# Rows and marks of batches 0 and 1 moved to GpSimd inside attention, and one square root placed three transfers later

## The reference, cut to what matters

```python
# B = 4 batches of N = 256 tokens, D = 256; 32 heads of 8; 32 experts, top 6, hidden width 176
x = x + tanh(g_xattn) * xattn(layernorm(x), ctx)     # rotary q and k, softmax over 256 keys, @ Wout + bout
x = x + tanh(g_ffn) * ffn(layernorm(x))
def ffn(flat):                                       # 1024 tokens
    shared = sum(relu(flat @ sw1[e] + sb1[e]) @ sw2[e] + sb2[e] for e in range(2)) / 2
    logits = flat @ router_w + router_b
    topk_p, topk_i = top_k(softmax(logits), 6);  topk_p /= topk_p.sum()
    routed = sum(gate[:, e] * (relu(flat @ rw1[e] + rb1[e]) @ rw2[e] + rb2[e]) for e in range(32))
    return shared + routed
```

## Time and profile before

| | us |
|---|---|
| median of 3 runs | 388.41 (388.39 to 388.55) |
| the profiled execution | 387.09 |
| its span, first to last instruction | 385.3 |
| busy: TensorE, VectorE, ScalarE, GpSimd | 333.4, 240.6, 214.6, 221.7 |

### The profile page before, as it was taken

The page is one execution under the profiler, slowest core; times in us unless marked ns, Lnnn a source line. Parts: engine busy times, 40 slices in busy tenths (PEclk is TensorE's granted clock), DMA queues, the critical chain, the costliest instruction groups (busy, mean ns, idle before and its releaser), DMA issues.

```text
span 385.3 us, 8620 instructions
## 1 busy us (share of the span) xinstructions
PE 333.4 (87%) x2574; PEld 262.3 (68%) x2574; DVE 240.6 (62%) x753; ACT 214.6 (56%) x537; POOL 221.7 (58%) x267
## 2 busy tenths in 40 slices
PE   8889999999899988786772999999999999999800
PEld 5567766666666664564541898999999999999700
DVE  7997788789789888569310355555555545445426
ACT  4795899979878877232130455555555555555400
POOL 8466332103013456757774288888788888787830
PEclk9999999999999999699786899999999999999965
DMA  7799999996004014613233488888888888897688
GB/s 227 208 309 310 308 326 315 320 237 205 4 2 134 19 60 125 204 60 117 101 116 125 128 125 144 137 151 138 139 146 147 142 143 141 138 146 108 76 195 282
DMA packets 63295, 62.20 MB, mean 161 GB/s; under 512 B 6258, under 2 KB 61588, under 8 KB 63252
## 3 DMA queue, kind: packets, MB, share of 16 engines
q1 hardware_dynamic: 48532, 44.60, 40.5%
q0 software_dynamic: 13680, 17.05, 27.4%
q10 hardware_dynamic: 1040, 0.01, 0.2%
HBM read 29.01 MB, written 32.63 MB: 160 GB/s over the span
## 4 chain that ended last, share of the span: by engine, by line
PE 55%; DVE 12%; issue 10%; POOL 9%; DMA 8%; ACT 5%; SPq 0%; POOLq 0%; DVEq 0%
PE psum L1608 14%; PE psum L1590 10%; POOL rows_by_block L502 7%; PE psum L1301 6%; PE psum L1348 5%; DVE nmax L906 5%; DMA sum<-ob,xs 5%; PE psum L1581 4%; PE psum L1599 3%; ACT probs L625 2%; PE psum L1319 2%; PE psum L1196 2%; PE psum L1282 2%; PE psum L1401 2%; POOL sum L546 2%
## 5 line engine op out<-in xcount | busy, mean ns | idle before, releaser
L546 POOL DMA_INDIRECT sum<-ob,xs x79 | 122.4, 1549 | 40.1 <-DVE ob L1166 26.9
L906 DVE TENSOR_REDUCE nmax<-psum 128x2 f32<-128x512 f32 x128 | 80.9, 683 | 13.2 <-PE psum L1301 12.3
L1608 PE MATMUL psum<-w,hT 88*128 (+1 forms) x316 | 81.5, 380 | 0.0
L625 ACT ACTIVATE probs<-psum 128x512 f32<-128x512 f32 x128 | 69.5, 599 | 15.3 <-PE psum L1319 13.8
L1166 DVE TENSOR_SCALAR ob<-psum,gate 128x256 f32<-128x256 f32 x79 | 38.2, 484 | 53.5 <-PE psum L1608 38.1
L755 ACT ACTIVATE hT<-psum,b1b 88x128 f32<-88x128 f32 x158 | 48.8, 357 | 35.6 <-PE psum L1599 34.6
L1590 PE MATMUL psum<-w,xT 128*128 x316 | 61.6, 318 | 0.3 <-ACT xT L746 0.3
L1608 PEld LDWEIGHTS psum<-w,hT 88*128 88x128 f32 (+1 forms) x316 | 53.8, 190 | 4.6 <-issue 0.3
L746 ACT ACTIVATE xT<-psum 128x256 f32<-128x256 f32 x79 | 30.3, 384 | 46.3 <-PE psum L1581 46.2
L502 POOL DMA_INDIRECT rows_by_block<-Vx,slot x48 | 47.6, 991 | 14.4 <-issue 14.1
L425 POOL CAST Qx<-nmax 128x8 fp32r<-128x8 f32 x32 | 6.3, 197 | 74.2 <-DVE nmax L906 74.1
(11 more groups left out here) (194 smaller groups left out, 468.6 us busy)
## 6 DMA issues: line engine op xcount, KB each, us to landing
rows_by_block<-blank SPq DMA_DIRECT2D x1, 10744.0 KB, 38.2
xs<-rows_by_block SPq DMA_DIRECT2D x79, 136.0 KB, 2.9
w<-in_L_ffn_rw_dram SPq DMA_DIRECT2D x2, 2816.0 KB, 22.1
w<-in_L_ffn_rw_dram SPq DMA_DIRECT2D x16, 352.0 KB
sum<-blank SPq DMA_DIRECT2D x3, 1152.0 KB, 13.4
w<-sum SPq DMA_DIRECT2D x12, 256.0 KB, 5.3
sum<-ob,xs POOLq DMA_INDIRECT x79
x_sb<-in_x_dram SPq DMA_DIRECT2D x4, 256.0 KB, 3.9
```

What stands on the lines that cost most here:

```text
L546: pool.indirect_dma_start(yd[i], bass.IndirectOffsetOnAxis(ap=xs[b % ROWS_AHEAD][:, X_ID:X_ID + 1].bitcast(U32), axis=0), ob[i][:, :], Non ...
L625: act.activation(probs[g % 2][:, :, n, :], st_bank(g, n)[:, :].rearrange("p (t q) -> p t q", t=TB), ACT.Exp, scale=SCALE).then_inc(exp_ok, 1)
L906: dve.tensor_reduce(nmax[i % 2][:, :, n], S_BANK[(4 * i + n) % SB][:, :].rearrange("p (t k) -> p t k", t=TB), AX.X, ALU.max, negate=True). ...
L1608: ins = pe.matmul(Y_BANK[b % 2][:, 0:D], hT[b % 2][0:rows, c, :], w2[0:rows, bass.ds(expert[b], 1), c, :].rearrange("p a n -> p (a n)"), s ...
```

## The change: what it does

In attention, for batches 0 and 1:

- The two normalised row tiles are made by GpSimd (`row_early`): the first right behind the Newton step at step 16 + 8b, the second behind the maxima of the next step. VectorE's two L945 at step 18 + 8b are gone.
- ScalarE copies the router's scores out of `T_BANK` into `lg` (`scores_copied`, semaphore `raw_ok`) ahead of its exponentials of step 21 + 8b. TensorE's next `transposes` waits for this copy and no longer for VectorE's sum. VectorE adds the bias from `lg` to `lg`.
- `mask` is made by GpSimd in three additions (`mask_early`, behind the maxima of step 22 + 8b, after a wait on `ch_ok`). VectorE's reduction L971 is gone, and so is its wait on its own `chosen`.
- The transfers inside attention are one fewer: step 30 issues one in place of two, and step 31 issues numbers 4 and 5 in place of 5 and 6.
- After attention, transfers 18, 19 and 20 stand ahead of the inverse root of batch 3, not behind it.

```diff
...
-            DEALT_AT = {28: (0, 2), 29: (2, 3), 30: (3, 5), 31: (5, 7)}
+            DEALT_AT = {28: (0, 2), 29: (2, 3), 30: (3, 4), 31: (4, 6)}
...
+                pool.wait_ge(nstep_ok, b + 1)
+                row_early(TB * b)
+
+            def row_early(n):
+                pool.wait_ge(pv_mm, NG)
+                pool.tensor_scalar(xrow[:, n, 0:D], x_sb[:, n, :], mv[:, n, 0:1], rstd[:, n:n + 1],
+                                   ALU.subtract, ALU.mult).then_inc(xn2_ok, 1)
+
+            def mask_early(b):
+                rows = slice(TB * b, TB * b + TB)
+                c = chosen[b]
+                some = halfsum[:, :, :, :]
+                pool.wait_ge(ch_ok, b + 1)
+                then(pool.tensor_tensor(some, c[:, :, 0:TOPK // 2, :], c[:, :, TOPK // 2:TOPK, :], ALU.add))
+                then(pool.tensor_tensor(mask[:, rows, :], some[:, :, 0, :], some[:, :, 1, :], ALU.add))
+                pool.tensor_tensor(mask[:, rows, :], mask[:, rows, :], some[:, :, 2, :], ALU.add).then_inc(mask_ok, 1)
...
+                    if g == NG * b + 17:
+                        row_early(TB * b + 1)
                     if g == NG * b + 21:
                         marks_of(b)
+                    if g == NG * b + 22:
+                        mask_early(b)
...
+            deal(EACH + EACH // 2, EACH + EACH // 2 + 3)
             inverse_root(B + 3, slice(NT - TB, NT))
-            deal(EACH + EACH // 2, NT * TOPK)
+            deal(EACH + EACH // 2 + 3, NT * TOPK)
...
+                if i - 1 in SCORE_STEPS:
+                    scores_copied(SCORE_STEPS[i - 1])
...
+            def scores_copied(b):
+                act.wait_ge(lg_mm, b + 1)
+                act.activation(lg[:, TB * b:TB * b + TB, :], C_LG[b].rearrange("p (t e) -> p t e", t=TB), ACT.Copy).then_inc(raw_ok, 1)
...
             def scores(b):
-                dve.wait_ge(lg_mm, b + 1)
-                dve.tensor_tensor(lg[:, TB * b:TB * b + TB, :], C_LG[b].rearrange("p (t e) -> p t e", t=TB),
+                if b < EARLY:
+                    dve.wait_ge(raw_ok, b + 1)
+                    src = lg[:, TB * b:TB * b + TB, :]
...
-                    if (at, part) == (18, 0):
-                        dve.wait_ge(nstep_ok, b + 1)
-                        dve.wait_ge(pv_mm, NG)
-                        normalised_row(TB * b)
-                    if (at, part) == (18, 2):
-                        normalised_row(TB * b + 1)
...
-                        then(choice_of(b))
-                    if (at, part) == (23, 0):
-                        mask_of(b)
+                        choice_of(b).then_inc(ch_ok, 1)
...
                 if i - AHEAD - 1 in SCORE_STEPS:
-                    pe.wait_ge(lg_ok, SCORE_STEPS[i - AHEAD - 1] + 1)
+                    pe.wait_ge(raw_ok, SCORE_STEPS[i - AHEAD - 1] + 1)
```

More of the change, by code:

```diff
@@ L166, in gated_cross_attention_moe @@
         roundup = blank[:, P:P + NE]
+        halfsum = placed[:, 0, :, :].rearrange("p k e -> p (k e)")[:, 0:TB * TOPK * NE // 4].bitcast(BF16).rearrange(
+            "p (t k e) -> p t k e", t=TB, k=TOPK // 2)
         HS_AT = 6 * H * HR
@@ L223, in gated_cross_attention_moe @@
             sem(n) for n in ("dif_ok", "ex_ok", "mask_ok", "masks_ok", "rk_mm", "row_ok", "slot_ok", "dealt"))
+        raw_ok, ch_ok = sem("raw_ok"), sem("ch_ok")
         nstep_ok, at8_ok, exp_row_ok, rk_ok, had_ok, upto_ok, placed_ok, pool_placed = (
@@ L942, in normalised_rows @@
                 normalise_rows(b, xrow[:, TB * b:TB * b + TB, 0:D], xn2_ok)
-            def normalised_row(n):
-                dve.tensor_scalar(xrow[:, n, 0:D], x_sb[:, n, :], mv[:, n, 0:1], rstd[:, n:n + 1],
-                                  ALU.subtract, ALU.mult).then_inc(xn2_ok, 1)
             def scores(b):
-                dve.wait_ge(lg_mm, b + 1)
-                dve.tensor_tensor(lg[:, TB * b:TB * b + TB, :], C_LG[b].rearrange("p (t e) -> p t e", t=TB),
+                if b < EARLY:
+                    dve.wait_ge(raw_ok, b + 1)
+                    src = lg[:, TB * b:TB * b + TB, :]
+                else:
+                    dve.wait_ge(lg_mm, b + 1)
+                    src = C_LG[b].rearrange("p (t e) -> p t e", t=TB)
+                dve.tensor_tensor(lg[:, TB * b:TB * b + TB, :], src,
                                   rtb_sb[:, :].unsqueeze(1).to_broadcast([P, TB, NE]), ALU.add).then_inc(lg_ok, 1)
```

## The result

| | before | after |
|---|---|---|
| median of the executions measured side by side, 20 each | 386.53 (383.21 to 389.02) | 388.94 (387.05 to 394.46) |
| the same, a second time (run g1, 23 and 12) | 387.58 | 388.08 (386.36 to 392.74) |
| the profiled execution, its span | 387.09, 385.3 | 387.26, 385.5 |
| mean granted clock of TensorE in the profiled execution | 0.948 | 0.959 |

The ratio of after to before is 1.0061, 95% interval [1.0036, 1.0087], and in the second measurement 1.0025 [0.9993, 1.0058]. The change cost between 0.25 and 0.6%, and by the second measurement alone a loss is not shown. From the 388.41 at which the prediction started, the first ratio gives 390.8 and the second 389.4, where 387.2 and "faster" were forecast. The ratios leave out the executions that took over 1.5% more than the quickest of the same kernel, among them the three of the changed kernel over 394.

What follows compares the result with a forecast made beforehand. The 79 blocks start only when all 48 transfers have landed, so time follows the last transfer. Attention 1.6 earlier, less one more transfer and a later root, put transfer 24 1.2 earlier: 388.41 - 1.2 = 387.2, range 386.2 to 389.0.

Steps and rivals of the forecast that it cites:

- The sum at step 31: All attention terms added at GpSimd's maxima of step 31: 1.6 earlier than 146.72.
- 18 to 19, rows gone from VectorE: Attention: two L945 leave VectorE, so TensorE's scores start 0.2 earlier.
- 21, the copy: Step 21: ScalarE's copy fits its idle time and removes TensorE's 0.84 wait; 0.7 gained (bounds 0.4 and 0.84).
- 23 and 24, the mask: VectorE loses L971 and comes earlier to the residual TensorE waits for; 0.4 gained.
- 24 to 26, wait for `had_ok`: VectorE stands still 1.2 ahead of the scan, having saved 0.64 by the rows; 0.6 lost.
- 28 to 31, batch 1: Steps 29 to 31: missing mask (0.7) and earlier residual (0.2) bring the maxima of step 31 0.9 earlier.
- Steps 24 to 26: the rows on GpSimd: Each row takes 0.95 (bounds 0.73 and 1.87); the second, ahead of the rounding, delays `had_ok`; 0.6 lost.
- rival A: GpSimd, steps 24 to 26: rows are slow, up to 1.87, sign turning at about 1.5; 389.4, chance 0.13.
- The transfers: After attention: one more follows (+1.28), the root starts at 169.4, transfer 24 goes 1.2 earlier, at 175.87.
- the new wait: GpSimd ahead of transfer 24: it waits about 1.3 for `slot` of batch 2, ready at 175.5.
- B: Steps 24 to 26: a row takes 0.4 to 0.5, the wait for `had_ok` hardly exists; 386.6, chance 0.17.
- C: Attention hardly gets faster, ScalarE having little idle time: 0.6 in place of 1.6; 388.2, chance 0.22.

Runs made afterwards that it cites:

- g1: The changed kernel measured again, nothing altered, against the kernel before; ratio 1.0025 [0.9993, 1.0058].
- e8: The kernel before with only ScalarE's copy of the router's scores added, TensorE waiting for that copy; ratio to before 0.9965 [0.9930, 1.0000].
- e2: The changed kernel with the root of batch 3 back ahead of transfer 18; ratio to the kernel before 1.0031 [0.9996, 1.0066].
- e4: The kernel before with two unread GpSimd operations ahead of the rounding at step 25; ratio to before 1.0113 [1.0078, 1.0148].
- g3: The changed kernel with batch 1's second row split, 128 columns on GpSimd, 128 on VectorE; ratio to before 1.0024 [0.9983, 1.0066].
- e3: The changed kernel with GpSimd's rounding ahead of the second row of batch 1; ratio to the kernel before 0.9985 [0.9955, 1.0015].
- e5: The changed kernel with rounding ahead of batch 1's second row and only transfer 18 ahead of batch 3's root; ratio to before 0.9913 [0.9880, 0.9947].
- e6: The kernel before with only transfer 18 moved ahead of the root of batch 3; ratio to before 0.9985 [0.9951, 1.0019].
- g2: Repeat: the changed kernel with rounding ahead of batch 1's second row and only transfer 18 ahead of batch 3's root; ratio to before 0.9890 [0.9843, 0.9938].
- e1: The kernel before with only the change's placement of transfers and of batch 3's root; ratio to before 1.0034 [0.9998, 1.0070].
- e7: The changed kernel with the row tiles back on VectorE, copy, mask and placement kept; ratio to the kernel before 0.9989 [0.9964, 1.0014].
- g4: Repeat: the changed kernel with GpSimd's rounding ahead of batch 1's second row, placement unchanged; one execution, 385.93.

## Why the prediction was wrong, point by point

**What bounds the kernel.** Right: time follows the last transfer, and the places named were the ones that moved. Between last transfer and end there are 177.5 to 179.8 us in the 14 profiles with no pattern by kernel, which is why spans follow the instants only to within 1 us.

**The sum at step 31** was to be -1.6 and was +0.36, a miss of 1.96. With 147.08 it met the prediction's own sign of being wrong, "after 146". Its terms (intervals between GpSimd's maxima, after against before):

| step of the prediction | forecast | measured |
|---|---|---|
| 18 to 19, rows gone from VectorE | 0.2 earlier | 0.07 earlier |
| 21, the copy | 0.7 earlier | 0.62 earlier (e8: 0.50) |
| 23 and 24, the mask | 0.4 earlier | 0.18 earlier |
| 24 to 26, wait for `had_ok` | 0.6 later | 1.04 later |
| 27 to 28, the clock | none | 1.10 later |
| 28 to 31, batch 1 | 0.9 earlier | 0.91 earlier |

**The step that failed** is "*Steps 24 to 26: the rows on GpSimd*", twice over. First in size: a row was taken at 0.95, nearest to L416, and took 1.23, inside the bounds of 0.73 and 1.87. The wait of the scan became 1.59 for 1.2, and steps 24 to 26 lost 0.44 more than forecast; by the prediction's own rate, 0.2 for each 0.1 of a row, the dearer row gives 0.56 of that kind. The Trainium skill (GPSIMD Engine Reference, section Engine selection) calls one-input work on GpSimd roughly line rate and two-input work about twice as slow as on VectorE. The traces disagree for this form: the one-input row took 1.23 on GpSimd, against 0.73 of the two-input L418, and VectorE had made the same row in 0.40 (L945 of the kernel before). Second in kind: the stall was priced as a stall and no more. The sum had no term for the clock. Behind the stall the granted clock fell to the lower rate, and that cost another 1.10. In all five profiles with a wait of 1.16 or more (after, e2, e4, g1, g3) the clock fell within 4.1 us of the wait's end, 1.6 to 3.2 us behind the end of TensorE's gap; in the nine others (a wait of 0.39 or less) it never did there. e3 shows the stall as the cause at this place: the same work in another order, and the gap and the fall are gone. So rival A had the right place and sign, but the wrong condition, "a row of about 1.5": a row of 1.23 was enough.

**The mask on GpSimd** was right: 0.55, 0.31 and 0.31, with gaps 1.3 for all (forecast 1.5), and no one waits for it. **Batch 1** came out as forecast in its sum, 0.91 for 0.9, and the choice at 141.38 waits for GpSimd's cast, as foreseen; how much of the 0.91 is the mask and how much the copy, no run separates.

**The transfers.** From the fills to the root 3.87 (3.8 forecast), from the root to `slot` 177.08 - 170.98 = 6.10 (6.09). Between the maxima of step 31 and the end of the fills lay 20.03; 19.19 before and 1.28 would be 20.47, so here 0.44 was won. The issue behind the wait took 0.79, not 0.4; the 0.74 of the earlier trace rows was near it. And 24 to 47 took 29.72 for 29.33, 0.39 more: transfer 25 takes 1.29 in place of 0.97, as in each profile in which transfer 24 waits for `slot` (1.10 to 1.30 in the seven of them). Together: 1.96 - 0.44 + 0.07 + 0.01 + 0.39 + 0.39 = 2.38, exactly the way from the forecast of -1.2 to the measured +1.18.

**The late root.** The prediction saw the new wait and held it to be harmless as long as attention gained. It was not: e5 differs from e3 in this alone, the ratio drops from 0.9985 to 0.9913, and the intervals do not meet (the two were measured in different sets). The variance is made at 166.4 to 170.4 (168.13 in the earlier trace rows; e4 and g1 aside, in which everything is late). How far it comes behind the maxima of step 31 goes with how long the clock is low between 155 and 171: 19.7 to 20.4 where it is low for 3.4 us (after, e4, e6), 21.2 to 22.0 where for about 6.8 (ten profiles), 22.2 where for 10.2 (e8). One transfer ahead of the root fills the wait mostly, and three overfill it.

**The rivals.** A came nearest. B (no wait) is what e3 made true by other means. C has some truth in the small terms: 0.43 of the 1.3 at steps 18 to 24 didn't come. The three small gains came at the waits that the forecast named, but were overrated, the mask's most (0.18 for 0.4).

**Where the expected gain went**, then: of the 2.38, 0.44 went to the longer stall at steps 24 to 26, 1.10 to the clock, 0.43 to overrated small terms, and a net 0.42 to the transfers. This is the account of one pair of profiles; whole executions vary by more than it. The ratios of e5 and g2 show that a gain of about 1% was there to be had.

## What to carry to other kernels

Before moving work onto a "free" engine, look at what stands behind it in that engine's order: an operation of 1.2 us cost nothing visible behind the semaphore that somebody waits for, and ahead of it 1.28 at once and 1.35 more by the clock (e3). In a loop that keeps TensorE nearly full, price a new gap with the clock that may fall behind it: here 1.35 to 1.5 us in the next step in four profiles, and more where the fall lasts longer (g1). And an instruction that heads a chain (the root) may stand behind just as much work as fits into the wait that it replaces, no more.

## What the runs showed of the hardware that I had not expected

- TensorE's granted clock fell from 1.00 to 0.50 in the middle of a loop in which it is busy for 25.25 of 26 us (94 to 120 in the changed kernel), behind gaps of 0.28 to 1.25 us, and came back after 3.4 us in three profiles, after 6.9 in e4 and after 17 in g1. The size of the gap does not decide it: the kernel before and those that keep its attention stand still for 0.83 or 0.84 at steps 21 and 29, and behind these eight gaps (before, e1, e4, e6) the clock fell twice, both times in e4. The Trainium skill (TensorE: Matmul & The Clock Gate, section A second HAM failure mode: psum-queue depth-cycling) tells of frequent small idle times between groups of matmuls that make the clock swing; here the falls followed a single such place. Other falls (from 105.2 in e5; from 135.2 to 137.8 in e7, e8, g3 and g4) begin 2 to 3 us behind the router's scores, with no gap of 0.2 or more ahead of them, in some executions of a program and not in others (g4 but not e3, e5 but not g2). What decides that is open.
- It shows in whole executions too: the median over executions of the mean granted clock is 0.937 and 0.943 for the changed kernel, 0.951 to 0.953 for the one before, 0.954 and 0.957 for e5 and g2. But e7, without the stall, has 0.944, e3 0.946, and e1 and e6, which leave attention as it was, 0.948 and 0.947, so the stall is not all that sets it. Among the 20 of the changed kernel, the eight at 0.942 or more took 387.05 to 388.0, the three at 0.921 or less over 394.
- GpSimd's subtraction and multiplication with two scalars per partition took 0.80 for 128 columns and 1.23 for 256, so by these two sizes about 0.37 of it would be fixed (an estimate).
- The first indirect transfer behind a wait on VectorE starts 0.79 after that result (177.08 to 177.87), against 0.30 between transfers that wait for nothing.
